# Evicting V on VectorE ahead of the maxima, and splitting the input tile by tile

## The reference

```python
h = shift_token(x)
qkv = h @ wqkv
q, k, v = jnp.split(qkv, 3, axis=-1)
...
q = l2norm(q) * qs
k = l2norm(k) * ksc
q, k = rotary_xpos(q, k)
o = local_attention(q, k, v)
o = o.transpose(0, 2, 1, 3).reshape(b, n, INNER)
x = x + o @ wo
```

## Time and profile before

| | us |
|---|---|
| median of 3 runs (lowest, highest) | 910.92 (910.48, 911.56) |
| the profiled execution | 909.12 |
| its span, first to last instruction | 907.3 |
| busy: TensorE, VectorE, ScalarE, GpSimd | 803.8, 677.0, 645.5, 531.6 |
| one step of the local attention, without / with a split | 7.93 / 9.33 |
| mean granted clock of TensorE | 0.98 |

### The profile page before, as it was taken

How to read it: one execution, slowest core, us unless ns; L and a number is a source line. 1 busy time by engine, 2 the same in 40 slices (tenths; PEclk the granted TensorE clock), 3 DMA queues, 4 the chain that set the end, 5 groups by cost and what they waited for, 6 DMA issues and landing times.

```text
span 907.3 us, 26209 instructions
## 1 busy us (share of the span) xinstructions
PE 803.8 (89%) x9912; PEld 616.1 (68%) x9912; DVE 677.0 (75%) x1389; ACT 645.5 (71%) x2037; POOL 531.6 (59%) x529
## 2 busy tenths in 40 slices
PE   4979999779999999999889887999999999988985
PEld 3558777557777777778766555777877777775652
DVE  4788898777887887787466767778787788746765
ACT  1217677579989899889743237988988998964463
POOL 1494233178888888888610008888888888951100
PEclk9999999989999999999999999999999999999998
DMA  7220001012222222222201122222222222222001
GB/s 272 73 52 4 3 4 41 3 48 54 51 64 57 60 51 63 53 63 54 60 19 24 23 52 54 63 55 57 58 61 56 62 51 61 57 51 100 0 35 58
DMA packets 64704, 48.24 MB, mean 53 GB/s; under 512 B 40410, under 2 KB 50948, under 8 KB 64068
## 3 DMA queue, kind: packets, MB, share of 16 engines
q1 hardware_dynamic: 64580, 46.57, 19.9%
HBM read 10.63 MB, written 2.10 MB: 14 GB/s over the span
## 4 chain that ended last, share of the span: by engine, by line
PE 55%; DVE 17%; ACT 17%; issue 7%; POOL 2%; DMA 1%; SPq 0%; DVEq 0%; POOLq 0%; ACTq 0%
PE ps L404 46%; PE ps L414 9%; ACT prob L862 6%; DVE nmax L1124 3%; ACT sq L804 3%; DVE nt L1152 2%; ACT V L831 2%; ACT oT L813 2%; DVE split L952 2%; ACT kT L838 1%; ACT pT L808 1%; DVE prob L1211 1%; DVE split L950 1%; ACT qT L823 1%; DVE vexp L1043 1%
## 5 line engine op out<-in xcount | busy, mean ns | idle before, releaser
L862 ACT ACTIVATE prob<-ps,nmax 128x128 f32<-128x128 f32 x512 | 181.8, 375 | 35.6 <-DVE nmax L1124 35.5
L404 PE MATMUL ps<-wqkv,split 128*128 128x512 f32 x576 | 186.8, 435 | 13.4 <-DVE split L952 9.9
L1349 POOL TENSOR_TENSOR prob<-prob,rinv 128x512 f32<-128x512 f32 x128 | 133.7, 1045 | 87.2 <-DVE rinv L1110 45.8
L404 PEld LDWEIGHTS ps<-wqkv,split 128*128 128x128 f32 x576 | 96.9, 194 | 32.5 <-DVE split L952 10.0
L1124 DVE TENSOR_REDUCE nmax<-ps 128x4 f32<-128x512 f32 x128 | 83.6, 686 | 47.0 <-PE ps L404 47.0
L414 PE MATMUL ps<-ident,prob 128*128 128x128 f32 x640 | 97.8, 276 | 14.1 <-POOL prob L1349 13.2
L862 ACT ACTIVATION_READ_ACCUMULATOR prob<-ps,nmax 128x1 f32 x512 | 109.2, 213 | 0.0
L1360 POOL TENSOR_TENSOR qr<-qr,ss 128x512 f32<-128x512 f32 x64 | 66.9, 1045 | 52.1 <-DVE qr L1136 52.1
L414 PEld LDWEIGHTS ps<-ident,prob 128*128 128x128 f32 x640 | 75.6, 141 | 28.3 <-POOL prob L1349 17.5
L404 PE MATMUL ps<-oT,wo 128*128 128x128 f32 x512 | 73.9, 287 | 22.2 <-ACT oT L813 22.2
L404 PEld LDWEIGHTS ps<-oT,wo 128*128 128x128 f32 x512 | 62.1, 191 | 37.5 <-ACT oT L813 36.5
(11 more groups left out here) (134 smaller groups left out, 1886.3 us busy)
## 6 DMA issues: line engine op xcount, KB each, us to landing
VB<-V SPq DMA_DIRECT2D x129, 128.0 KB, 2.4
kT<-kT SPq DMA_DIRECT2D x65, 128.0 KB, 2.4
XS<-X SPq DMA_DIRECT2D x32, 128.0 KB, 2.3
XS<-X SPq DMA_DIRECT2D x128, 32.0 KB, 1.9
D<-in_xT SPq DMA_DIRECT2D x8, 256.0 KB, 4.9
XS<-in_xT SPq DMA_DIRECT2D x2, 1024.0 KB, 6.3
out_T<-XS SPq DMA_DIRECT2D x8, 256.0 KB, 2.0
raw<-in_wqkv SPq DMA_DIRECT2D x2, 768.0 KB, 3.9
```

Source lines behind the costliest of these rows:

```text
L404: return nc.tensor.matmul(o, l, r, start=start, stop=stop, skip_group_check=True)
L862: nc.scalar.activation(prob[:, par, grp, s * P:(s + 1) * P], ps[:, 4 + grp, s * P:(s + 1) * P], ACT.Exp, bias=nmax[:, par, grp * 4 + s:grp ...
L1349: g.tensor_tensor(p4, p4, rinv[:, slot, 4 * grp:4 * grp + 4].unsqueeze(2).broadcast_to([P, 4, P]), ALU.mult).then_inc(l_prob, 1)
```

## The change

Three edits. The eviction of V leaves ScalarE and becomes a copy on VectorE behind the two sums of squares and in front of the first maximum, with the same waits. The split of the input is no longer made for four tiles between the maxima, but for one tile (n+3) in each step: the high part between the two sums of squares, the low part behind the second. TensorE's wait in front of the first projection counts tiles instead of chunks. TensorE's own order stays.

```diff
@@ TensorE, local(n)
                     if live(n, 2, TILES):
-                        pe.wait_ge(l_split, L * CHUNKS + (n + 2) // TPC + 1)
+                        pe.wait_ge(l_split, base + n + 3)
                         wait(pe, l_qm, base + n + 2)
                         project(0, *now, l_qk)
@@ ScalarE, local(n), behind qT
-                    if live(n, 0, TILES):
-
-                        act.wait_ge(l_v, base + n + 1)
-                        wait(act, l_o, base + n - 1)
-                        if live(n, -1, TILES):
-                            act.wait_ge(v_prev[nxt], 32 * ((base + n - 1) // 2 + 1))
-                        nc.scalar.activation(V[:, par, :], ps[:, 2, :], ACT.Copy).then_inc(l_ve, 1)
@@ VectorE
-            def split_into(slot, src, width, made, value):
-
-                hi, lo = split[:, slot, 0, 0:width], split[:, slot, 1, 0:width]
-                v.tensor_copy(hi, src).then_inc(split_hi, 1)
-                dve.wait_ge(split_hi, value + 1)
-                v.tensor_tensor(lo, src, hi.bitcast(F32), ALU.subtract).then_inc(made, 1)
@@ VectorE, local(n)
                         wait(dve, l_floor, base + n + 2)
                         v.tensor_reduce(nt[:, 0:8], hd(sq[:, 0, :]), AX_X, ALU.add)
+                    if live(n, 3, TILES):
+                        m = n + 3
+                        wait(dve, l_v, base + m - 2 * TPC + 1)
+                        x_m, slot, cols = shifted(XS[0], m, P), (m // TPC) % 2, bass.ds((m % TPC) * P, P)
+                        v.tensor_copy(split[:, slot, 0, cols], x_m).then_inc(split_hi, 1)
+                    if live(n, 2, TILES):
                         dve.wait_ge(l_sq, 2 * (base + n + 2) + 2)
                         v.tensor_reduce(nt[:, 8:16], hd(sq[:, 1, :]), AX_X, ALU.add).then_inc(l_norm, 1)
+                    if live(n, 3, TILES):
+                        dve.wait_ge(split_hi, base + m + 1)
+                        v.tensor_tensor(split[:, slot, 1, cols], x_m, split[:, slot, 0, cols].bitcast(F32),
+                                        ALU.subtract).then_inc(l_split, 1)
+                    if live(n, 0, TILES):
+                        dve.wait_ge(l_v, base + n + 1)
+                        wait(dve, l_o, base + n - 1)
+                        if live(n, -1, TILES):
+                            dve.wait_ge(v_prev[nxt], 32 * ((base + n - 1) // 2 + 1))
+                        v.tensor_copy(V[:, par, :], ps[:, 2, :]).then_inc(l_ve, 1)
                     maxima(0)
-                    if live(n, 3, TILES) and (n + 3) % TPC == 0:
-                        j = (n + 3) // TPC
-                        if j > 1:
-                            dve.wait_ge(l_v, base + n + 3 - TPC)
-                        split_into(j % 2, shifted(XS[0], j, CHUNK), CHUNK, l_split, L * CHUNKS + j)
                     maxima(1)
```

## The result

The changed kernel takes 1141.4 us (median of 4 runs, 1135.6 to 1142.9) against 910.7: ratio 1.254, 95% interval 1.248 to 1.260. The forecast was 1142. The profiled execution took 1135.6, with a span of 1133.8 and a mean granted clock of 0.909; the other three had clocks of 0.905 to 0.899, and a further execution, which the median leaves out, took 1148.8 at 0.893.

The account below looks back on a forecast made before the run. The step was read as a loop through VectorE, ScalarE and TensorE, without slack at the third projection's wait for the eviction. 909.1 - 19.6 + 194.4 + 56 = 1139.9, 1142 us against the median before; range 1072 to 1175.

Parts of the forecast that it names:

- The count and the place: TensorE's third projection waits for VectorE's late eviction in steps 0 to 29 of each layer, 60 times.
- The splits: Splits between VectorE's maxima go: 14 of 16, 1.40 us each, 19.6 us less; starts of layers put at nothing.
- no wait: TensorE's first projection needs its own tile's split, made a step earlier, so it was to wait for none.
- The eviction's delay: Third projection starts at 266.33 instead of 263.09, 3.24 us later in 60 steps: 194.4 us more, bounds 180 and 238.
- rival E: TensorE's head start, no 0.4 wait for oT, shortens steps: 24 us less, 1118; no chance of its own.
- The lock of VectorE and GpSimd: The 128-column difference waits for GpSimd's running kA product, ending near 265.64; undisturbed 0.28 would give 3.0 per step.
- The clock: TensorE's 3 us gaps bring the 1.2 GHz clock in 43 of 60 steps, 1.3 us each: 56 us more.
- the mean clock: Sign in the profile after: the granted clock's mean below 0.90.
- A: TensorE's clock holds despite the gaps: 1086 us, or 1072 with the undisturbed difference too; chance 0.20.
- B: Every TensorE gap costs a slow spell, 60 instead of 43: 1164 us; chance 0.20.
- C: GpSimd shuts VectorE out for one more instruction each step: 44 more, 1186 us, 1208 with every gap cold; chance 0.09.
- D: The eviction's wait does not hold TensorE at the third projection and the kernel gets faster, 891 us; chance 0.02.

Follow-up runs that it names:

- The early place of the eviction: Changed kernel with VectorE evicting V ahead of the rotated Q (tA) instead of behind the second sum of squares: 919.9 us, ratio 1.013.
- the late projection: Changed kernel with TensorE's third projection and its wait for the eviction moved behind the scores: 947.1 us, ratio 1.041.
- The split alone: Changed kernel with the eviction of V back on ScalarE and the per-tile split kept on VectorE: 891.1 us, ratio 0.982.
- the run with the extra products: Changed kernel with eight unused 512-column products on TensorE ahead of its wait for the eviction, steps 1 to 29 of each layer: 1081.9 us, ratio 1.191.
- the eviction alone: Kernel before with only the eviction of V moved to VectorE ahead of the first maximum, four-tile split kept between the maxima: 1128.2 us, ratio 1.244.

## Why the prediction was right, point by point

**The count and the place.** 60 waits of TensorE for the eviction were forecast and 60 are there. The early place of the eviction takes the wait away, the late projection leaves a wait of 1.14 with nothing behind it that the step hangs on, and each takes most of the loss with it.

**The splits.** -19.6 forecast. The split alone gives 891.1 against 908.3 on the same chip, -17.3, with an interval of -14.4 to -18.5 us. In the middle steps the cover was there: with the split alone the 56 of them take 444.9 us together against 464.7, 19.8 less. The missing 2 us stand where I had put nothing, at the start of the layers. In the first layer it takes 25.5 us instead of 22.1 from the first projection to the first middle reciprocal; there, with the split alone, a projection waits 1.94 for the split (at 185.95), and the slow clock lasts longer: from 188 to 192 us the granted clock was 0.53, before it was 1.00. I had allowed 2 us either way for this; which of the two costs it was not tried. In the changed kernel TensorE waits 3 times for a split, 5.6 us in all, where I had said "no wait".

**The eviction's delay.** 3.24 forecast, 194.4 in all. The undisturbed step grew from 7.93 to 11.02, by 3.09, or 185 us. On the clock of the earlier trace rows the second sum was placed 6.70 behind the first maximum and stands at 6.56 (280.34 to 286.90). Of these 0.14, 0.05 is TensorE's head start: it waits 0.15 for oT instead of 0.39 and turns K 4.80 behind the first maximum (285.14) instead of 4.85. That is rival E in a small form; I had said it would give nothing. The other 0.09 is ScalarE: the squares of K, which the sum waits for, take 0.59 (at 286.28) where they took 0.68. The low half was put at 0.42 and costs 0.43 from the end of the sum to its own (287.59 to 288.02); the run with the eviction ahead of it says 0.43 too. The copy from PSUM takes 0.68 for the 0.69 taken from the maximum.

**The lock of VectorE and GpSimd.** L1147 started at 287.50 and ended 288.02, as the earlier trace rows had it: behind kA, whose end is 287.89, by 0.13. The 0.28 of a free instruction would have made the term too small by 14 us. The rule in the Trainium skill ("SBUF — State Buffer", "Who interferes with whom") that the two engines' instructions exclude each other for a whole instruction held here, and the runs add a price: the rounding copy took 1.09 and 1.13 us behind a GpSimd product against 0.19 alone. In the changed kernel itself the copy comes 0.17 ahead of kA (286.45 and 286.62) and takes 0.29 (once 1.20, at 443.78). I had let it push kA by 0.1. It escaped by a narrow lead; the early eviction moved it to the other side of the start of kA, and that cost 30 us (919.9 against 890.0).

**The clock.** 43 steps with the clock down at 1.3 us, 56 us forecast; 42 such steps, 1.38 above the undisturbed ones, 58 us; and 59.6 by the run with the extra products. Here the match is closer than the reasoning deserves: five of seven gaps in the earlier trace rows was a small sample, and the runs show that the share does not follow from the gap alone (below). One sign was missed: the mean clock was to be below 0.90 and is 0.909 in the profiled execution, 0.899 to 0.905 in the other three.

**The sum.** In the profiled executions the span grew by 226.5. 185 - 17 + 58 = 226. Of 1142 against 1141.4 the terms were each off by 2 to 9 us, and the errors cancelled. A match within 1 us is luck for another reason too: the executions of this one kernel lie between 1135.6 us at a mean clock of 0.909 and 1148.8 at 0.893, longer with each step down of the clock, so the clock's term alone moves by more than that.

**The rivals.** A and B bracket the clock term and the 42 of 56 lies between: 14 gaps of 2.9 us were followed by no slow clock, which is against B and what was drawn from the clock's default for it; C (VectorE shut out for another instruction) did not happen in the low half, which was 0.52 or less in nearly all steps; D would have needed the eviction 2.9 us earlier, and the kernels that do evict early show that D was a matter of places on VectorE's queue: with the eviction alone early 919.9 us, with the rounding copy early too 890, where D said 891.

## What to carry to other kernels

When an eviction changes engines, read which queue the freed bank's next writer stands in and what is queued behind that writer; the eviction must end before that point of the step, and here the second sum and the low half ahead of it were worth 1.3 us times 60, the whole loss was 231. Give each part of a change its own run: half of this one was worth 17 us and was buried under the other half. A small VectorE instruction that reads SBUF twice, or rounds from SBUF to SBUF, has the price of the GpSimd instruction that it meets (the rounding copy 0.19 us alone, 1.09 to 1.22 behind kA), so place it where GpSimd waits.

## What was not expected of the hardware

The clock does not follow from the length of the gap. In the changed kernel the gap of 2.93 us ahead of 277.66 was followed by full speed and the one of 2.94 ahead of 288.69 by 0.50, as the stretches further up show. Behind the first of them (stretches, the same columns):

```profile
278.00:279.00 1.00, 1.00 (x9) 0.69 (x8) 0.00 (x0) 0.00 (x0) 0.92 (x2) 1.00 0.23 55
279.00:280.00 1.00, 1.00 (x34) 0.93 (x36) 0.00 (x0) 0.90 (x3) 0.63 (x1) 1.00 0.34 76
280.00:281.00 1.00, 0.84 (x17) 0.60 (x10) 0.66 (x2) 0.57 (x2) 0.00 (x0) 1.00 0.00 0
```

With the eviction alone or ahead of the low half nearly all gaps are shorter, 2.49, yet the clock fell in 53 and 51 of 56 steps, against 42 with the longer ones. Timeline of TensorE with the eviction alone, in a step in which it fell:

```profile
296.81 0.96 PE L404 MATMUL ps<-wqkv,split 128*128 128x512 f32 x3 [2.49 <-DVE V L1151]
```

Nor are the outcomes scattered: in the changed kernel every fourth or fifth step (in one place every second) is undisturbed, and those between take mostly 12.0, 12.5 and 12.4 in turn. Filling 2.1 of the 3 us removed the slow clock from all 56. What decides between such gaps was not settled by these runs.
